# Routing steps of two mixture-of-experts layers inside the stages ahead of them

## The chip, the cores and the metric

The kernel runs on one core of a Trainium2 chip. The metric is the device time of one execution in microseconds (us), the median of several runs.

## The reference

The input is 2 x 2048 tokens of 256 float32 values. Four residual layers follow each other, each on the layer-normalised rows: an attention with 16 heads, a feed-forward, a memory-routed gated linear attention, and the same feed-forward again:

```python
x = x + attn_a(layernorm(x))
x = x + ffn(layernorm(x))
x = x + attn_b(layernorm(x))
x = x + ffn(layernorm(x))
```

The feed-forward is a mixture of 16 experts of inner width 128, two per token, and one shared expert:

```python
shared = silu(x @ ws_gate) * (x @ ws_up) @ ws_down
scores = sigmoid(x @ gate_w.T)
topk_w, topk_idx = top_k(scores, 2)
topk_w = topk_w / (topk_w.sum(-1, keepdims=True) + 1e-20) * 2.5
out = shared + sum over the two of topk_w * expert[topk_idx](x)
```

The last part of attn_b, which the output stage computes, is for each token a sum of two memories' results and the shared one, divided by its root mean square over each head's 64 values, times silu of a gate (x @ w_g), times w_o.

## The kernel before

The tokens are 32 tiles of 128 rows; four tiles (512 tokens) are a step, so a pass over all tokens has 8 steps. The program is a row of stages, one function each, in which every engine has an in-order program of its own; semaphores order them, and all engines meet between two stages. Four stages matter here.

**Merge** (phase_merge, L990) ends attn_a. It works in 16 half-steps of two tiles: PE makes the linear part's outputs, transposes and projects, DVE adds the residual, POOL multiplies the states. Beside it, four steps of rows are already normalised for the feed-forward (DVE L1096 ff., POOL, ACT).

**The feed-forward** (phase_moe, L1181) runs twice: the first time its names begin with m1_ or m_ and four steps (K) come normalised, the second time one (K = 1). Its front goes through the 8 steps. For each, PE transposes the rows (L1584), makes the 16 logits of each row (L1594) and the gate/up product of the shared expert (L1604); ACT copies the transposed rows (L1390), normalises the rows of a later step (L1374), takes silu (L1382) and an exponential (L1396), with a table load ahead of each of the two; DVE picks the two best experts (L1456 to L1487); PE counts the rows ahead in each expert (the ranks, L1615 to L1619); DVE makes the slots (L1490 to L1499); POOL then scatters the rows into the experts' regions in DRAM (L1358). For each token tile and choice there is one indirect store, eight a step, and a step's first waits until all earlier ones have landed:

```python
if n:
    pool.wait_ge(sent, n * G * TOPK * 16)
for t in range(n * G, (n + 1) * G):
    for j in range(TOPK):
        pool.indirect_dma_start(out=xs, ...)
```

When all steps are counted, DVE makes the tables of tiles (L1507 to L1535). Sixteen stores of blank rows fill each region's end, eight issued by SP (L1281) and eight by ACT (L1405), where they stand behind the last silu. Then SP loads the experts' tiles (L1292), after waits for the tables, all scatters and all blank stores, and 79 tiles go through the experts (L1667 to L1689).

**The output stage** (phase_final, L2742) ends attn_b in 8 steps and lies right ahead of the second feed-forward. DVE mixes the rows (L2866, tile fn_o), PE makes the gates (L2923), ACT takes silu of 1024 columns (L2824) and 16 squares with sums (L2831), POOL turns the sums into an inverse root (L2803, L2807), DVE multiplies (L2875, L2883), PE transposes (L2933), ACT copies (L2843), PE projects (L2945), DVE adds to the residual (L2892). Each engine's loop over the steps is written out by hand, with silu and squares two steps ahead. When all is done, the rows of step 0 are normalised: sums on DVE (L2907, L2910), the scaling on POOL (L2809 to L2815), ACT (L2849).

The order of the engines' work is what the program says; no planner is in it.

## Time and profile before

| what | value |
|---|---|
| median of 3 runs | 2501.88 us (2498.71 to 2502.81) |
| profiled execution | 2522.7 us |
| its span | 2521.0 us |
| mean granted PE clock | 0.92 |
| busy PE, PEld | 2123.9 us (84%), 1629.8 us (65%) |
| busy DVE, ACT, POOL | 1816.8 us (72%), 1546.2 us (61%), 1521.3 us (60%) |

The merge takes 1080 to 1141 us of the span, the first feed-forward follows; the output stage goes from 2141 to 2226, the second feed-forward's front from there to 2342 and its experts to the end. Busy shares are averages over stages with different limits, so each stage is read by itself. PE is TensorE, PEld its weight loads, DVE VectorE, ACT ScalarE, POOL GpSimd, SP the engine that only issues transfers.

### The profile page before, as it was taken

The page shows a single profiled execution, that of the slowest core. Times are in us where ns is not written, and L with a number is a line of the kernel's source. Part 1 is how long each engine was busy: PE and PEld are TensorE (multiplying, and loading weights), DVE is VectorE, ACT ScalarE, POOL GpSimd, SP SyncE. Part 2 cuts the span into 40 slices and gives each one's busy share as a digit, 9 for nine tenths or more (in the row PEclk, how much of TensorE's full clock was granted, in tenths as well). Part 3 has the DMA queues.
Part 4 walks back from the last instruction along what each step waited for, and adds up shares of the span by engine and source line. Part 5 has one row for each costly group of instructions (what it writes and reads, how often), then busy time and mean ns, then how long its engine had stood idle before and what let it go on. Part 6 is the DMA issues. An engine that isn't in the chain of part 4 may idle for free. (4 is left out here: it accounts for less than half of the span.)

```text
span 2521.0 us, 107266 instructions
## 1 busy us (share of the span) xinstructions
PE 2123.9 (84%) x43952; PEld 1629.8 (65%) x43952; DVE 1816.8 (72%) x4507; ACT 1546.2 (61%) x3824; POOL 1521.3 (60%) x3168
## 2 busy tenths in 40 slices
PE   8789999999999999988499443899999997876893
PEld 5557777777767777765378342677767765654782
DVE  6689999989989998846355552677777775764456
ACT  5578889988888988824233221566766664653330
POOL 3367778877878887885545365454445444356452
PEclk9989999999999999998799655899999998888896
DMA  6911111111121111134466443111111110733456
GB/s 214 281 53 43 47 48 47 43 50 43 46 76 50 43 43 50 24 127 164 114 216 208 165 159 118 31 52 50 54 49 51 43 35 30 250 147 115 143 149 227
DMA packets 188837, 245.65 MB, mean 97 GB/s; under 512 B 41673, under 2 KB 144982, under 8 KB 187457
## 3 DMA queue, kind: packets, MB, share of 16 engines
q1 hardware_dynamic: 161824, 182.08, 24.1%
...
q14 instruction: 132, 1.07, 0.1%
...
## 5 line engine op out<-in xcount | busy, mean ns | idle before, releaser
L672 ACT ACTIVATE at_E<-at_S,at_mn 128x1024 f32<-128x1024 f32 (+7 forms) x704 | 592.1, 847 | 58.9 <-DVE at_mn L741 45.6
L741 DVE TENSOR_REDUCE at_mn<-at_S 128x1 f32<-128x1024 f32 (+3 forms) x448 | 484.5, 1100 | 6.2 <-PE at_S L851 5.8
L892 PE MATMUL at_pcs<-at_E,at_c 128*32 128x256 f32 (+1 forms) x4864 | 410.6, 339 | 2.5 <-issue 2.4
L851 PE MATMUL at_S<-am_sk,am_sq 96*32 96x512 bf16 (+3 forms) x4608 | 375.3, 348 | 9.3 <-ACT at_E L672 2.3
L609 POOL TENSOR_TENSOR at_kvo<-am_kh,am_vh 128x256 f32<-128x256 f32 x512 | 304.8, 629 | 0.1
L892 PEld LDWEIGHTS at_pcs<-at_E,at_c 128*32 128x32 f32 x4864 | 227.1, 109 | 27.1 <-issue 5.4
L1363 POOL DMA_INDIRECT expert_out<-m_ysb,m_dst x158 | 155.4, 984 | 133.7 <-issue 75.2
L594 POOL TENSOR_TENSOR at_half<-at_half 128x128 f32<-128x128 f32 (+4 forms) x640 | 185.5, 290 | 50.1
L662 ACT ACTIVATE at_Tt<-at_S,at_mn 128x192 f32<-128x192 f32 x512 | 174.1, 431 | 59.9 <-DVE at_mn L729 59.8
L851 PEld LDWEIGHTS at_S<-am_sk,am_sq 96*32 96x32 bf16 x4608 | 146.6, 97 | 81.1 <-ACT at_E L672 31.7
L892 PE MATMUL at_pcs<-at_Tt,at_c 128*32 128x128 f32 x1024 | 177.9, 275 | 0.9 <-issue 0.9
L1675 PE MATMUL m_b<-m_wgu,m_xT 128*128 x632 | 167.9, 389 | 1.3 <-issue 0.8
L2612 PEld LDWEIGHTS gl_S<-gl_X,gl_Y 32*64 32x64 f32 x8448 | 110.4, 133 | 82.1 <-issue 62.5
L729 DVE TENSOR_REDUCE at_mn<-at_S 128x4 f32<-128x768 f32 x128 | 121.7, 951 | 51.3 <-PE at_S L834 50.7
L869 PE MATMUL at_M<-am_ident,at_Tt 128*32 128x64 f32 x8192 | 150.9, 221 | 8.5 <-issue 3.2
L2612 PE MATMUL gl_S<-gl_X,gl_Y 32*64 32x32 f32 (+1 forms) x8448 | 130.6, 226 | 31.7 <-ACT gl_A L2336 16.4
L869 PEld LDWEIGHTS at_M<-am_ident,at_Tt 128*32 128x32 f32 x8192 | 134.0, 110 | 33.2 <-issue 26.8
L1416 ACT ACTIVATE m_sg<-m_b 128x128 f32<-128x128 f32 x158 | 43.8, 277 | 170.7 <-issue 109.0
L672 ACT ACTIVATION_READ_ACCUMULATOR at_E<-at_S,at_mn 128x1 f32 x704 | 144.9, 206 | 0.0
L1675 PEld LDWEIGHTS m_b<-m_wgu,m_xT 128*128 128x128 f32 x632 | 120.2, 194 | 23.5 <-issue 6.8
...
L1550 DVE TENSOR_TENSOR m_hd<-m_sg,m_b 128x128 f32<-128x128 f32 x158 | 45.4, 287 | 109.4 <-ACT m_sg L1416 103.4
...
## 6 DMA issues: line engine op xcount, KB each, us to landing
...
rt_yin<-expert_out SPq DMA_DIRECT2D x7, 1024.0 KB, 12.3
...
```

Source lines behind the costliest of these rows:

```text
L594: pool.tensor_tensor(half[:, :, 0:w], half[:, :, 0:w], half[:, :, w:2 * w], ALU.add).then_inc(s_half, 1)
L609: ins = pool.tensor_tensor(kvo[:, t, 0:DH * DH].rearrange("p (d e) -> p d e", d=DH), k3[:, t, :].unsqueeze(2).to_broadcast([P, DH, DH]), v ...
L662: ins = nc.scalar.activation(Tt[:, q, s, :], S[v % NS_B][:, at:at + TW], ACT.Exp, bias=mn[:, q, s, 0:1], scale=-1.0)
L672: ins = nc.scalar.activation(E[:, at:at + w], S[v % NS_B][:, i * CW:i * CW + w], ACT.Exp, bias=mn[:, q, s, 1 + j:2 + j], scale=-1.0, accum ...
L729: nc.vector.tensor_reduce(mn[:, g % NQ, :, 0].rearrange("p (b s) -> p b s", b=2), S[v % NS_B][:, :].rearrange("p (b c) -> p b c", b=2)[:, ...
L741: nc.vector.tensor_reduce(mn[:, q, :, :].rearrange("p s k -> p (s k)")[:, at[0]:at[0] + 1], S[v % NS_B][:, 0:w], AX.X, ALU.min).then_inc(s ...
L851: ins = nc.tensor.matmul(S[v % NS_B][x, at:at + cw], sq[:, u, t * P + x.start:t * P + x.stop], sk[:, u, c0 + c:c0 + c + cw], start=True, s ...
L869: ins = nc.tensor.matmul(M[x, s * P + e * SEG:s * P + (e + 1) * SEG], Tt[:, q, s, e * SEG + x.start:e * SEG + x.stop], ident[:, e * SEG:(e ...
L892: ins = nc.tensor.matmul(pcs[j * R:(j + 1) * R, cols[0]:cols[1]].rearrange("p (b c) -> p b c", c=P), lhsT, rhs, start=(n, j) not in touche ...
L1363: pool.indirect_dma_start(out=yb.rearrange("t (j d) -> (t j) d", j=TOPK), out_offset=bass.IndirectOffsetOnAxis(ap=dst[:, t, :], axis=0), i ...
L1675: ins = nc.tensor.matmul(bank[4 + t % 2][:, 0:2 * MH], xT[:, t % 2, k, :], wgu[:, k, ds(at, D)], start=(k == 0), stop=(k == KC - 1))
L2612: return nc.tensor.matmul(out, Y[r_h, i % 2, l, u * P + keys:u * P + keys + out.shape[0]], queries, start=True, stop=True)
```

## The change

The routing of a step (logits, exponential, pick, ranks, slots, scatter) and its constants move out of phase_moe into a class Routing, which two stages share. Four numbers say how it is split: routed (steps that the earlier stage routes), ahead (steps that it normalises), begun (steps that it scatters), and turns (the order in which the feed-forward goes through the steps for the shared expert and the routings left).

- Merge routes step 0 and normalises four steps as before, each one iteration earlier; it scatters nothing: (1, 4, 0, turns 1 to 7, then 0).
- The output stage routes steps 0 to 4, normalises 0 to 5 and scatters 0 to 3: (5, 6, 4, turns 5, 6, 0, 7, 1, 2, 3, 4). The second feed-forward routes steps 5, 6, 7 and scatters 4 to 7.
- In the output stage each engine's order changes: the gates product and its silu are split in two halves in three buffers of 512 columns, with work on routed rows between them; the stage also loads the routing weights, which phase_moe did.
- In phase_moe the tables (tables(), the same instructions as before) are made right behind step 7's routing.

```diff
...
+class Routing:
...
+        self.routed, self.ahead, self.begun, self.turns = routed, ahead, begun, turns
...
+    def constants(self, pool):
+        pool.iota(self.iota_i[:, :], pattern=[[1, NE]], base=0, channel_multiplier=0).then_inc(self.made, 1)
...
+    def logits(self, pe, n, rows_T, p_l):
+        if n:
+            pe.wait_ge(self.s_ex, n)
+            pe.wait_ge(self.s_chain, (n - 1) * self.CH + 9)
+        for t in range(GT):
+            for k in range(KC):
+                ins = self.nc.tensor.matmul(p_l[:, t * NE:(t + 1) * NE], rows_T[:, k, t * P:(t + 1) * P], self.gw[:, k, :],
+                                            start=(k == 0), stop=(k == KC - 1))
...
+    def exps(self, act, n, p_l):
+        act.wait_ge(self.s_log, n + 1)
+        if n:
+            act.wait_ge(self.s_chain, (n - 1) * self.CH + 1)
+        self.nc.scalar.activation(self.ex[:, :, :], p_l.rearrange("p (g e) -> p g e", g=GT), ACT.Exp, scale=-1.0
+                                  ).then_inc(self.s_ex, 1)
...
+    def pick(self, dve, n):
...
+        dve.wait_ge(self.s_ex, n + 1)
...
+    def scatter(self, pool, n, a, z):
+        if a == 0:
+            pool.wait_ge(self.s_e2, n + 1)
+            pool.wait_ge(self.s_slot, n + 1)
+            if n:
+                pool.wait_ge(self.sent, n * GT * TOPK * 16)
+        for t in range(n * GT + a, n * GT + z):
+            for j in range(TOPK):
+                pool.indirect_dma_start(out=self.xs, out_offset=bass.IndirectOffsetOnAxis(ap=self.slot[:, t, j:j + 1], axis=0),
+                                        in_=self.hx[:, t, :], in_offset=None).then_inc(self.sent, 16)
...
-                if n >= 8 and n % 2 == 0 and (n - 8) // 2 < K:
-                    scale_of((n - 8) // 2)
+                if n == 3:
+                    rt.constants(pool)
+                if n >= 6 and n % 2 == 0 and n // 2 - 3 < rt.ahead:
+                    scale_of(n // 2 - 3)
...
+                if n >= 6 and n % 2 == 0 and n // 2 - 3 < rt.routed:
+                    turned(n // 2 - 3, 1)
+                if n >= 7 and n % 2 and (n - 7) // 2 < rt.routed:
+                    rt.exps(act, (n - 7) // 2, p_l)
+                if n >= 5 and n % 2 and (n - 5) // 2 < rt.ahead:
...
+                    if k < rt.routed:
+                        turned(k, 0)
...
+                if n >= 8 and n % 2 == 0 and (n - 8) // 2 < rt.routed:
+                    rt.place(dve, (n - 8) // 2, p_c)
                 add_rows(n)
-                if n >= 2 and n % 2 == 0 and n // 2 - 1 < K:
+                if n >= 2 and n % 2 == 0 and n // 2 - 1 < rt.ahead:
                     stats_of(n // 2 - 1)
+                if n >= 7 and n % 2 and (n - 7) // 2 < rt.routed:
+                    rt.pick(dve, (n - 7) // 2)
...
+                k = (n - 8) // 2
+                if n >= 8 and n % 2 == 0 and k < rt.routed:
+                    rt.ranks(pe, k, p_c)
                 if n + 1 < NS:
                     turn(n + 1)
+                k = (n - 5) // 2
+                if n >= 5 and n % 2 and k < rt.routed:
+                    turn_rows(k, 0)
                 project(n)
...
+                if n >= 5 and n % 2 and k < rt.routed:
+                    turn_rows(k, 1)
+                k = (n - 6) // 2
+                if n >= 6 and n % 2 == 0 and k < rt.routed:
+                    if k == 0:
+                        pe.wait_ge(rt.gate_in, 16)
+                    pe.wait_ge(s_rT, KC * (k + 1))
+                    rt.logits(pe, k, rT, p_l)
...
-        SETS = ((1, 2), (2, 4), (4, NS)) if K == 1 else ((4, 6), (6, NS))
+        TURNS = rt.turns
+        SETS = ((K, (K + NS) // 2), ((K + NS) // 2, NS))
...
-            for n in range(NS):
-                if n == 1:
+            for n in range(rt.begun, NS):
+                if n == rt.begun + 1:
                     scale_of(LAST)
                 if n >= K:
                     pool.wait_ge(s_hn, (n + 1 - K) * G)
-                pool.wait_ge(s_e2, n + 1)
-                pool.wait_ge(s_slot, n + 1)
-                if n:
-                    pool.wait_ge(sent, n * G * TOPK * 16)
...
+                rt.scatter(pool, n, 0, G)
...
+            for i, n in enumerate(TURNS):
                 for k in range(KC):
-                    act.wait_ge(s_T, n * KC + k + 1)
-                    if k == 0 and n >= 2:
-                        act.wait_ge(s_gu, n - 1)
-                    nc.scalar.copy(hT[:, u, k, :], p_T[k][:, :]).then_inc(s_hT, 1)
-                if n + 1 < NS and n + 1 >= K and n:
-                    front(n + 1)
-                if n:
-                    silu(n - 1)
-                act.wait_ge(s_log, n + 1)
-                nc.scalar.activation(ex[:, :, :], p_l[:, 0:G * NE].rearrange("p (g e) -> p g e", g=G), ACT.Exp,
-                                     scale=-1.0).then_inc(s_ex, 1)
-                if n == 0 and K == 1:
-                    front(1)
+                    act.wait_ge(s_T, i * KC + k + 1)
+                    if k == 0 and i >= 2:
+                        act.wait_ge(s_gu, i - 1)
+                    nc.scalar.copy(hT[:, i % 2, k, :], p_T[k][:, :]).then_inc(s_hT, 1)
+                if i + 1 < NS and TURNS[i + 1] >= K:
+                    front(TURNS[i + 1])
+                if i:
+                    silu(i - 1)
+                if n >= rt.routed:
+                    rt.exps(act, n, p_log)
             silu(NS - 1)
...
+            for i, n in enumerate(TURNS):
+                if i:
+                    hidden(i - 1)
+                if n >= rt.routed:
+                    rt.pick(dve, n)
+                    rt.place(dve, n, p_rank)
+                if i == 0:
                     for later in range(*SETS[LAST]):
                         stats_of(later)
                 else:
-                    add_shared(n - 1)
...
+                    add_shared(i - 1)
+                if n == NS - 1:
+                    tables()
...
+            for i, n in enumerate(TURNS):
+                pe.wait_ge(s_hT, (i + 1) * KC)
+                if n >= rt.routed:
+                    rt.logits(pe, n, hT[:, i % 2, :, :], p_log)
+                if i + 1 < NS:
+                    turn(i + 1)
+                if i:
+                    shared_down(i - 1)
+                if n >= rt.routed:
+                    rt.ranks(pe, n, p_rank)
+                if n == NS - 1:
+                    pe.wait_ge(rt.s_run, NS)
+                    pe.wait_ge(rt.s_ex, NS)
+                    nc.tensor.matmul(p_l[:, 0:NE], rt.ones_h[:, :], rt.run[:, NS % 2, :], start=True, stop=True
+                                     ).then_inc(s_n, 1)
+                if i == 0:
                     pe.wait_ge(shared_in, 32)
-                if n + 1 < NS:
-                    shared_gu(n)
-            pe.wait_ge(s_run, NS)
-            pe.wait_ge(s_ex, NS)
-            nc.tensor.matmul(p_l[:, 0:NE], ones_h[:, :], run[:, NS % 2, :], start=True, stop=True).then_inc(s_n, 1)
-            shared_gu(NS - 1)
+                shared_gu(i)
...
+            inverse(0)
+            inverse(1)
+            rt.constants(pool)
+            for n in range(1, NS):
+                if n + 1 < NS:
+                    inverse(n + 1)
+                if n - 1 < rt.ahead:
+                    scale_of(n - 1)
+                if 0 <= n - 3 < rt.begun:
+                    rt.scatter(pool, n - 3, 0, G)
...
             for n in range(NS):
                 for k in range(KC):
                     act.wait_ge(s_T, n * KC + k + 1)
                     if k == 0 and n:
                         act.wait_ge(s_zmm, 2 * n)
                     nc.scalar.copy(yT[:, k, :], p_T[:, k, :]).then_inc(s_yT, 1)
+                if 0 <= n - 2 < rt.routed:
+                    rt.exps(act, n - 2, p_l)
                 if n + 2 < NS:
-                    gates(n + 2)
+                    gates(n + 2, 0)
+                if 0 <= n - 1 < rt.ahead:
+                    front(n - 1)
+                if 0 <= n - 1 < rt.routed:
+                    turned(n - 1, 0)
+                    turned(n - 1, 1)
+                if n + 2 < NS:
+                    gates(n + 2, 1)
                     squares(n + 2)
-            act.wait_ge(s_rstd, 4)
-            for a in range(G):
...
             mix(1)
             for n in range(NS):
+                norm(n)
+                if 0 <= n - 3 < rt.routed:
+                    rt.place(dve, n - 3, p_c)
+                if n:
+                    residual(n - 1)
+                    if n - 1 < rt.ahead:
+                        stats_of(n - 1)
                 if n + 1 < NS:
                     gate_rows(n + 1)
-                norm(n)
+                if 0 <= n - 2 < rt.routed:
+                    rt.pick(dve, n - 2)
                 if n + 2 < NS:
                     mix(n + 2)
-                if n:
-                    residual(n - 1)
...
+            for n in range(2):
+                gates(n, 0)
+                gates(n, 1)
             for n in range(NS):
                 turn(n)
+                if 0 <= n - 2 < rt.routed:
+                    if n == 2:
+                        pe.wait_ge(rt.gate_in, 16)
+                    rt.logits(pe, n - 2, rT, p_l)
                 if n + 2 < NS:
-                    gates(n + 2)
+                    gates(n + 2, 0)
                 project(n)
+                if 0 <= n - 1 < rt.routed:
+                    turn_rows(n - 1, 0)
+                    turn_rows(n - 1, 1)
+                if n + 2 < NS:
+                    gates(n + 2, 1)
+                if 0 <= n - 2 < rt.routed:
+                    rt.ranks(pe, n - 2, p_c)
...
-        phase_merge(nc, a["x"], q_full, Y, kvc, q0, x0, wc_s, kv_dram, own, state, keep, hx, 4)
-        phase_moe(nc, Y, tw, a["f_gate"], a["f_wgu"], a["f_wd"], xs, yb, gx, None, "m1_", hx, 4)
+        rt = Routing(nc, shared, "r1_", hx, tw, xs, 1, 4, 0, (1, 2, 3, 4, 5, 6, 7, 0))
+        phase_merge(nc, a["x"], q_full, Y, kvc, q0, x0, wc_s, kv_dram, own, state, keep, hx, rt, a["f_gate"])
+        phase_moe(nc, Y, tw, a["f_wgu"], a["f_wd"], xs, yb, gx, None, "m1_", hx, rt)
...
-        phase_final(nc, Y, hT_dram, o_dram, yb, ident, wg, won, tw_b, hT, hx)
-        phase_moe(nc, Y, tw, a["f_gate"], a["f_wgu"], a["f_wd"], xs, yb, None, a["out"], "m2_", hx, 1)
+        rt = Routing(nc, shared, "r2_", hx, tw, xs, 5, 6, 4, (5, 6, 0, 7, 1, 2, 3, 4))
+        phase_final(nc, Y, hT_dram, o_dram, yb, ident, wg, won, tw_b, hT, hx, rt, a["f_gate"])
+        phase_moe(nc, Y, tw, a["f_wgu"], a["f_wd"], xs, yb, None, a["out"], "m2_", hx, rt)
...
```

ACT in the output stage, before: two steps (fn_p_g are the gates, fn_o the mixed rows, fn_p_T the transposed ones).

```order
L2824 ACTIVATE fn_silu<-fn_p_g 128x1024
L2831 ACTIVATE fn_sq,fn_ss<-fn_o 128x64 x16
L2843 COPY fn_yT<-fn_p_T 128x512 x2
L2824 ACTIVATE fn_silu<-fn_p_g 128x1024
L2831 ACTIVATE fn_sq,fn_ss<-fn_o 128x64 x16
L2843 COPY fn_yT<-fn_p_T 128x512 x2
```

And in the changed kernel, one step from the third on (r_ex is the exponential of the routing, ready_rows are the normalised rows, fn_rT their transposed form):

```order
L2966 COPY fn_yT<-fn_p_T 128x512 x2
L1065 ACT_TABLE_LOAD
L1065 ACTIVATE r_ex<-fn_lc 128x64
L2932 ACT_TABLE_LOAD
L2932 ACTIVATE fn_silu<-fn_p_g 128x512
L2952 ACTIVATE ready_rows<-stream,fn_nbias,fn_rstd 128x256 x4
L2959 COPY fn_rT<-fn_p_T 128x512 x2
L2932 ACTIVATE fn_silu<-fn_p_g 128x512
L2940 ACTIVATE fn_sq,fn_ss<-fn_o 128x64 x16
```

The normalising of a finished step's rows and the copies of their transposes now stand between the first half of silu and the second, with the 16 squares behind; a table load precedes the exponential and the silu behind it.

POOL in the output stage, before: its last two inverses and the scaling.

```order
L2803 TENSOR_SCALAR fn_var<-fn_ss 128x16
L2807 TENSOR_TENSOR fn_inv<-fn_var,fn_half 128x16
L2803 TENSOR_SCALAR fn_var<-fn_ss 128x16
L2807 TENSOR_TENSOR fn_inv<-fn_var,fn_half 128x16
L2809 TENSOR_SCALAR fn_varied<-fn_mv 128x4
L2811 TENSOR_TENSOR fn_rstd<-fn_varied,fn_half 128x4
L2813 TENSOR_TENSOR fn_shift<-fn_mv,fn_rstd 128x4
L2815 TENSOR_SCALAR fn_nbias<-fn_shift 128x4
```

And in the changed kernel, one of the middle steps:

```order
L2908 TENSOR_SCALAR fn_var<-fn_ss 128x16
L2912 TENSOR_TENSOR fn_inv<-fn_var,fn_half 128x16
L2897 TENSOR_SCALAR fn_varied<-fn_mv 128x4
L2899 TENSOR_TENSOR fn_rstd<-fn_varied,fn_half 128x4
L2901 TENSOR_TENSOR fn_shift<-fn_mv,fn_rstd 128x4
L2903 TENSOR_SCALAR fn_nbias<-fn_shift 128x4
L1144 DMA expert_rows<-ready_rows,r_slot 67712x258 x8
```

The scaling, which stood once at the end, stands behind each inverse of the first steps, and eight stores of routed rows follow it; the next inverse comes after them.

## Rows read from the trace of the kernel before

**Rows 1.** Windows view, three stretches: start:end, us, busy (and count) of PE, PEld, DVE, ACT, POOL, ...
```profile
1080.00:1141.00 61.00, 56.66 (x458) 45.40 (x450) 29.45 (x66) 17.64 (x33) 44.87 (x50) 0.94 0.39 130
...
2141.00:2226.00 85.00, 68.77 (x320) 57.81 (x320) 57.01 (x104) 50.12 (x285) 28.60 (x21) 0.91 0.56 186
...
2226.00:2342.00 116.00, 77.82 (x365) 52.21 (x365) 62.78 (x316) 49.50 (x77) 72.24 (x94) 0.82 0.44 153
```

**Rows 2.** Timeline of POOL, second feed-forward: store 1, store 17, store 57, store 64 (start, us)
```profile
2238.61 1.11 POOL L1358 DMA_INDIRECT expert_rows<-ready_rows,m_slot  x1 [4.25 <-DVE m_slot L1499]
...
2265.40 0.96 POOL L1358 DMA_INDIRECT expert_rows<-ready_rows,m_slot  x1 [2.30 <-DMA expert_rows<-ready_rows,m_slot]
...
2326.71 0.96 POOL L1358 DMA_INDIRECT expert_rows<-ready_rows,m_slot  x1 [3.03 <-DMA expert_rows<-ready_rows,m_slot]
...
2335.56 0.96 POOL L1358 DMA_INDIRECT expert_rows<-ready_rows,m_slot  x1 [0.30 <-issue]
```

**Rows 3.** Timeline of SP's and ACT's queues: stage start, ACT's blank stores, first expert load
```profile
2226.39 0.35 SPq L1270 DMA_DIRECT2D m_gw<-in_f_gate  x1
...
2321.65 9.87 ACTq L1405 DMA_DIRECT2D expert_rows<-m_empty  x8
...
2338.79 19.97 SPq L1292 DMA_DIRECT2D m_xg<-expert_rows  x15
```

**Rows 4.** Timeline of PE, second feed-forward: first product, a settled step, the last
```profile
2238.26 5.07 PE L1604 MATMUL m_b<-m_hT,m_wgu 128*128 128x512 f32 x8
...
2259.57 3.68 PE L1604 MATMUL m_b<-m_hT,m_wgu 128*128 128x512 f32 x8
2263.09 1.85 PE L1594 MATMUL m_b<-m_gw,m_hT 128*128 128x16 f32 x16
2264.79 1.07 PE L1584 MATMUL m_b<-m_ident,ready_rows 128*128 128x128 f32 x8
2265.70 1.89 PE L1631 MATMUL m_b<-m_wd,m_hid 128*128 128x256 f32 x8
...
2314.79 0.20 PE L1615 MATMUL m_b<-m_sel,m_tri_h 128*128 128x64 bf16 x1 [3.12 <-DVE m_sel L1479]
...
2315.33 5.38 PE L1604 MATMUL m_b<-m_hT,m_wgu 128*128 128x512 f32 x8
```

**Rows 5.** Timeline of POOL, output stage: inverses of steps 6 and 7, the scaling
```profile
2205.73 0.20 POOL L2803 TENSOR_SCALAR fn_var<-fn_ss 128x16 f32<-128x16 f32 x1 [4.70 <-ACT fn_sq L2831]
2206.01 3.12 POOL L2807 TENSOR_TENSOR fn_inv<-fn_var,fn_half 128x16 f32<-128x16 f32 x1
...
2213.84 0.20 POOL L2803 TENSOR_SCALAR fn_var<-fn_ss 128x16 f32<-128x16 f32 x1 [4.71 <-ACT fn_sq L2831]
...
2221.30 0.25 POOL L2809 TENSOR_SCALAR fn_varied<-fn_mv 128x4 f32<-128x4 f32 x1 [4.27 <-DVE fn_mv L2910]
...
2223.03 0.23 POOL L2815 TENSOR_SCALAR fn_nbias<-fn_shift 128x4 f32<-128x4 f32 x1
```

**Rows 6.** Timeline of ACT, second feed-forward: normalising, silu, table load, exponential
```profile
2250.89 2.08 ACT L1374 ACTIVATE ready_rows<-stream,m_nbias,m_rstd 128x256 f32<-128x256 f32 x4
...
2254.28 0.60 ACT L1382 ACTIVATE m_act_g<-m_b 128x512 f32<-128x512 f32 x1
2254.89 1.28 ACT L1396 ACT_TABLE_LOAD   x1
2256.19 0.22 ACT L1396 ACTIVATE m_ex<-m_b 128x64 f32<-128x64 f32 x1
```

**Rows 7.** Timeline of PE, output stage: gates product and projection
```profile
2172.80 3.62 PE L2923 MATMUL fn_p_g<-ready_wg,ready_hT 128*128 128x256 f32 x16
2176.26 3.62 PE L2945 MATMUL fn_p_z<-ready_won,fn_yT 128*128 128x256 f32 x16
```

**Rows 8.** Tile fn_o: duration ns min/median/max of ACT's squares
```profile
L2831 ACT ACTIVATE fn_sq<-fn_o x128: 238/243/257, 2152.6 to 2213.4; 128x64 f32<-128x64 f32 x128
```

**Rows 9.** Timeline of POOL, first feed-forward: its first scatter
```profile
1154.90 1.22 POOL L1358 DMA_INDIRECT expert_rows<-m_rows,m_slot  x1 [5.57 <-DVE m_slot L1499]
```

476 lines of the change are left out of this document (251 added, 225 removed).

## The prediction

> **What bounds the kernel now.** I read the windows view first, then POOL's timeline in the second feed-forward, then the timelines of its neighbours. The windows [rows 1] are to show where an engine fills its stretch: PE works 56.66 of the merge's 61 us and 68.77 of the output stage's 85, so these two are PE's or nearly so; in the second feed-forward's front nobody fills the time, POOL is busy 72.24 of 116 us and PE 77.82. There an order of waits sets the end.
>
> In the front that order is POOL's [rows 2]. It scatters the rows of one step after the other, eight sets of eight indirect stores. The first store starts at 2238.61, the last at 2335.56; between sets it waits 2.30 us for the earlier ones to land, and from 2265.40 to 2326.71 five sets take 12.26 us each. The expert loads follow at 2338.79, 112.4 us after the stage's start at 2226.39 [rows 3]. They also wait for 16 stores of blank rows; ACT issues half of them, in 9.87 us, and only behind its last silu. They end at 2331.5, under the scatters.
>
> PE works in the same stretch [rows 4]: the first shared gate/up product starts at 2238.26, the last at 2315.33, so a step takes 11.0 us. A settled step is shorter: 3.52 us for the product (2259.57 to 2263.09), 1.70 logits (to 2264.79), 0.91 transposes (to 2265.70), 1.73 down, some 0.8 waiting for the pick (both estimates, from 1.89 less an overlap, and from the step's rest), 0.15 ranks: 8.8. The other 2.2 us a step are waits and a slower clock: after 3.12 us idle the product takes 5.38 us instead of 3.68. The granted clock of the front is 0.82, of the output stage 0.91 [rows 1], so PE spends part of both at the lower level, 1.2 GHz.
>
> In the output stage one step takes 8.11 us (2205.73 to 2213.84) [rows 5]. POOL is idle 4.7 us of it, waiting for ACT's squares; what fills it is PE, with a gates product of 3.46 and a projection of 3.62 [rows 7] and 0.91 for transposes.
>
> **The change, part by part.** First the second feed-forward's front. Four sets leave it, and of the routings three remain (steps 5, 6, 7). POOL needs 4 x 12.26 = 49 us, starting about 4.5 us in, so it ends at 54 and binds nothing. PE takes its place. I leave the first product where it is, 11.9 us in. The seven intervals to the last product: two with routing at 8.8, five without at 3.52 + 0.91 + 1.73 + 0.55 waiting for the hidden rows (an estimate) = 6.7, together 51.1. Of the excess of 2.2 us a step (15.4) I take half, 7.7, because five of seven steps lose the wait for the pick, in which PE cooled. Bounds: none and all of it. Then 3.5 for the product and 0.6 for silu, and now ACT's eight blank stores lie bare: 9.9, and 2.3 to land. First expert load at 11.9 + 51.1 + 7.7 + 16.3 = 87.0 instead of 112.4: **25.4 us gained**, bounds 17.7 and 33.1. So of the 49 us taken off POOL some half comes through; the next lateness is PE's steps and ACT's stores.
>
> Second, the output stage. What matters is not that POOL and ACT have room but the loop that the new order closes. ACT normalises step n-1 (front) ahead of the second half of silu and of the squares of step n+2; POOL takes the inverse of n+2 from those squares, and the scaling, on which the next front waits, stands behind that inverse. One turn of the loop is:
> - inverse 3.40 (2205.73 to 2206.01 + 3.12) and scaling 1.96 (2221.30 to 2223.03 + 0.23) on POOL [rows 5];
> - four normalisations, 2.08 on ACT [rows 6];
> - eight transposes, 0.91 [rows 4], then the second half of the gates product, 3.46 / 2 = 1.73, on PE [rows 7]: in PE's order it stands behind those transposes;
> - silu of 512 columns 0.60 [rows 6], and 16 squares of 0.243 = 3.9 on ACT [rows 8].
>
> That is 14.6, and 14.9 with some seven handovers of 0.05 us. Before, the loop held only squares, inverse, product and transposes, and its step was 8.11. The two copies of 512 columns (0.60 each, as the silu of that width), two table loads, exponential and first silu half (1.2 + 2.56 + 0.22 + 0.60 = 4.6) fit under the inverse and scaling (5.36) and cost nothing; without that cover they would cost 4.6 us a step. POOL's scatter takes 9.81 (2326.71 to 2335.56 + 0.96); it lies beside front to squares (9.3 plus handovers), so it adds little: POOL's own turn is 3.40 + 1.96 + 9.81 = 15.2. Ahead of the routed transposes PE waits for the front some 3 us, by my layout of the step, the length after which it was slow [rows 4]. Then 2.64 us of the loop take up to twice as long. I take 14.9 for the first turn and 16.6 for four; bounds 14.9 and 17.5 for all five. From the inverse of step 2 to that of step 7 are five turns: 81.3 instead of 5 x 8.11 = 40.6, **40.7 us lost**. At the end the last inverse, scaling and scatter take 15.2 and 1.8 to the next stage, 17.0 instead of 12.55 (2213.84 to 2226.39) [rows 3]: 4.4 lost. At the start the constants and the stats of step 0 delay the inverse of step 2 by some 2.2 (bounds 1 and 3). Output stage: **47.3 us lost**, bounds 40 and 55.
>
> The scatter stores share the DMA with the stage's loads, and the mean 0.56 busy share of the stage [rows 1] leaves room; I cost them at nothing. The loads' cover is the longer step itself.
>
> A table load costs 1.28 here, and the next activation starts 0.02 us after it (2254.89 + 1.28, 2256.19) [rows 6]: no wait of its own behind it. The Trainium skill, page "ScalarE: Activation LUTs", section "What ACT_TABLE_LOAD costs", counts a drain of about the load's own length as well, 2.66 us a switch. By the row the two loads cost nothing; by that rule they would overrun their cover, which speaks against the change, and it is a rival below.
>
> Third, merge and first feed-forward. Merge is PE's: 1.70 + 0.91 + 0.15 and 0.7 for waits, 3.5 lost; the constants on POOL lie in the slack between two states (bounds 2.5 and 7). In the feed-forward POOL's first scatter no longer waits 5.57 us for the pick [rows 9]; all eight sets stay, and POOL stays the bound: 5.6 gained (bounds 3 and 10, as ACT's stores now meet other sets). Net **2.1 gained**.
>
> Sum: 47.3 - 25.4 - 2.1 = **+19.8 us**. The profiled execution took 2522.7 us, 0.8% above the median of 2501.88, so it would come to 2542.5; on the median it is 2521.7, and I forecast 2522.
>
> **The rivals.**
> *It comes out even.* The clock stays high in the output stage (14.9 x 5 = 74.5, 33.9 lost, and 4.4 and 1.0 at the ends: 39.3), the front's stalls vanish with the scatters (33.1 gained), and the first half gains 5. Then 39.3 - 33.1 - 5 = +1: 2503. For it: PE would have only short waits outside the one for the front. Against it: that wait is about as long as the one that slowed PE here.
>
> *Faster.* The loop doesn't bind, because squares get ahead by more than a step, and the added work lies beside the old. Then a turn is the busiest engine's: PE 68.77 / 8 + 2.8 + the part at low clock, ACT 50.12 / 8 + 2.08 + 2.56 + 0.22 + 1.2 = 12.3, and POOL 15.2 where it scatters. Two turns of 12.3 and three of 15.2 are 70.2, 29.6 lost, 34.0 with the end; with 33.1 and 7 gained elsewhere: 2496. It decides where the mean turn is below about 14.2 us. Against it: every link waits in an in-order queue.
>
> *Tables.* A switch costs ACT twice what a load shows, 2.56 us instead of 1.28, because the engine empties around it. Then ACT's work under POOL's 5.36 us is 4.6 + 2.56 = 7.2, so 1.8 too long, five times: 9 us more, 2531. Against it: between the end of the normalising (2250.89 + 2.08 = 2252.97) and the silu (2254.28) lie 1.31 us, one load and no more [rows 6]. The page of the Trainium skill named above states such a drain.
>
> *A stall more.* If PE's unexplained 2.2 us a step come with the scatters, four steps of the output stage have them too: 9 more, 2531. This lies in the range.
>
> **How the numbers follow.** Forecast with its own bounds 0.74, tables 0.03, even 0.12, faster 0.11. About 5 us (0.2%) is what a measurement of this kernel can tell from none. The lower end takes the output stage's lower bound with the front's upper and the first half at its best (10 - 2.5 = 7.5 gained): 40 - 33.1 - 7.5 = -0.6, 2501, which takes in the even case. The upper end leaves the first half as forecast: 55 - 17.7 - 2.1 = 35, 2537. What it leaves out is the faster case and a few in 100 of the others. Slower: 0.74 + 0.03 and 0.01 of the even case, 0.78; the same 0.11; faster 0.11.
>
> **What would show it.** In the changed profile: the inverse (fn_inv) of steps 3 to 7 every 15 to 17 us, each waiting for fn_sq; the output stage 130 us long, ending with eight scatters; PE idle about 3 us ahead of the transposes of routed rows; the first expert load of the second feed-forward some 87 us after its start, with ACT's blank stores just ahead of it and POOL long idle; the first feed-forward's first scatter some 6 us in. I am wrong if fn_inv comes every 12 us or less, or if the expert loads start before 75 us.

## The result and the profile after

The changed kernel takes 2523.72 us (median of 4 runs, 2519.0 to 2525.07), the kernel before 2500.88 beside it: 1.0088 times as long, 95% interval 1.0071 to 1.0106, or 22.8 us slower. The forecast was 2522.

The two profiled executions differ by 1 us alone (spans 2521.0 and 2522.0), since the one before was a long one. A second profile of the kernel before (b0, below) has a span of 2499.8 and shows where: 15 us of it lie between the first feed-forward's expert loads and the output stage, which the change does not touch, and 5 in the last experts. All differences below are against this second profile. The stages are cut at rows of the timelines: a feed-forward begins where POOL clears its identity (m_ident) and its front ends with the first expert load, the output stage begins with the first load of fn_o (for merge, that of mg_qT).

| us | merge | first front | between | output stage | second front | last experts |
|---|---|---|---|---|---|---|
| before, first profile | 57.3 | 118.8 | 880.0 | 84.6 | 112.4 | 182.2 |
| before, second profile | 57.6 | 116.5 | 864.8 | 84.8 | 114.9 | 177.2 |
| changed | 67.2 | 110.9 | 862.8 | 138.8 | 80.6 | 175.9 |
| changed less second | +9.6 | -5.6 | -2.0 | +54.0 | -34.3 | -1.3 |

With 1.8 us ahead of merge this is the 22.2 us between the spans. The spread of one stage from profile to profile is of the order of 2.5 us: the output stage, which x2 and m1 below leave as it is, takes 136.2 and 138.3 us there instead of 138.8. The bounds of the last two stages, from SP's timeline of the changed kernel and then of the kernel before (start, duration, engine; the next stage before began at 2207.7):

```profile
2126.74 0.33 SPq L2870 DMA_DIRECT2D fn_o<-o_shared  x1
...
2265.50 0.56 SPq L1448 DMA_DIRECT2D m_wgu<-in_f_wgu  x1
...
2346.12 52.90 SPq L1469 DMA_DIRECT2D m_xg<-expert_rows  x36
```

```profile
2122.90 0.33 SPq L2779 DMA_DIRECT2D fn_o<-o_shared  x1
...
2322.62 6.46 SPq L1292 DMA_DIRECT2D m_xg<-expert_rows  x6
```

POOL's timeline in the output stage of the changed kernel answers to [rows 5]. Each fn_var row is the start of a step's inverse, from step 2 to step 7:

```profile
2161.04 0.32 POOL L2908 TENSOR_SCALAR fn_var<-fn_ss 128x16 f32<-128x16 f32 x1 [8.42 <-ACT fn_sq L2940]
...
2176.76 0.20 POOL L2908 TENSOR_SCALAR fn_var<-fn_ss 128x16 f32<-128x16 f32 x1 [9.52 <-ACT fn_sq L2940]
...
2192.94 1.00 POOL L2908 TENSOR_SCALAR fn_var<-fn_ss 128x16 f32<-128x16 f32 x1 [11.01 <-ACT fn_sq L2940]
2194.02 2.93 POOL L2912 TENSOR_TENSOR fn_inv<-fn_var,fn_half 128x16 f32<-128x16 f32 x1
2196.93 0.24 POOL L2897 TENSOR_SCALAR fn_varied<-fn_mv 128x4 f32<-128x4 f32 x1
...
2199.39 1.11 POOL L1144 DMA_INDIRECT expert_rows<-ready_rows,r_slot  x1 [0.23 <-issue]
...
2202.32 1.62 POOL L1144 DMA_INDIRECT expert_rows<-ready_rows,r_slot  x1 [0.30 <-issue]
...
2210.36 0.93 POOL L2908 TENSOR_SCALAR fn_var<-fn_ss 128x16 f32<-128x16 f32 x1
...
2227.77 0.91 POOL L2908 TENSOR_SCALAR fn_var<-fn_ss 128x16 f32<-128x16 f32 x1
...
2245.18 0.58 POOL L2908 TENSOR_SCALAR fn_var<-fn_ss 128x16 f32<-128x16 f32 x1
```

The five turns take 15.7, 16.2, 17.4, 17.4 and 17.4 us. In the second profile of before the same six lie between these two rows, 8.1 apart:

```profile
2154.60 0.20 POOL L2803 TENSOR_SCALAR fn_var<-fn_ss 128x16 f32<-128x16 f32 x1 [7.55 <-ACT fn_sq L2831]
...
2195.18 0.20 POOL L2803 TENSOR_SCALAR fn_var<-fn_ss 128x16 f32<-128x16 f32 x1 [4.70 <-ACT fn_sq L2831]
```

Two things are to be seen. In the first two turns POOL waits 9.5 and 11.0 us for ACT's squares: it is not the bound there. In the last three no idle time stands behind fn_var: POOL comes from its last store straight to the next inverse, so it is the bound itself. The row at 2192.94 opens such a turn: inverse 3.99 (to 2196.93), scaling 2.46 (to 2199.39), eight stores 10.97 (to 2210.36). Beside two of its long rows DVE runs a product over 1024 columns:

```profile
2192.68 1.20 DVE L3003 TENSOR_TENSOR fn_gated<-fn_o,fn_silu 128x1024 f32<-128x1024 f32 x1
...
2201.88 1.22 DVE L3011 TENSOR_TENSOR fn_y<-fn_gated,fn_inv 128x1024 f32<-128x1024 f32 x1
```

ACT's timeline in the same turn, and PE's in two others, show the other chain:

```profile
2193.82 1.28 ACT L1065 ACT_TABLE_LOAD   x1
2195.12 0.22 ACT L1065 ACTIVATE r_ex<-fn_lc 128x64 f32<-128x64 f32 x1
2195.36 1.28 ACT L2932 ACT_TABLE_LOAD   x1
2196.66 0.60 ACT L2932 ACTIVATE fn_silu<-fn_p_g 128x512 f32<-128x512 f32 x1
2199.20 2.08 ACT L2952 ACTIVATE ready_rows<-stream,fn_nbias,fn_rstd 128x256 f32<-128x256 f32 x4 [1.95 <-POOL fn_nbias L2903]
...
2205.86 0.60 ACT L2932 ACTIVATE fn_silu<-fn_p_g 128x512 f32<-128x512 f32 x1 [2.76 <-PE fn_p_g L3059]
```

```profile
2184.09 1.09 PE L3091 MATMUL fn_p_T<-ready_ident,ready_rows 128*128 128x128 f32 x8 [2.69 <-ACT ready_rows L2952]
2185.03 3.39 PE L3059 MATMUL fn_p_g<-ready_wg,ready_hT 128*128 128x256 f32 x8
...
2218.73 1.38 PE L3091 MATMUL fn_p_T<-ready_ident,ready_rows 128*128 128x128 f32 x8 [3.75 <-ACT ready_rows L2952]
2219.91 3.32 PE L3059 MATMUL fn_p_g<-ready_wg,ready_hT 128*128 128x256 f32 x8
```

ACT waits 1.95 us for the scaling, normalises, and later waits 2.76 us for the second half of the gates product. PE waits 2.69 and 3.75 us for the normalised rows, long after its projection, and then needs 3.4 and 3.3 us for that half, which takes 1.89 at the high clock (2192.41 in x3 below). The granted clock of the stage is 0.86 (0.91 before, [rows 1]), by the windows view:

```profile
2127.00:2265.00 138.00, 93.81 (x465) 78.12 (x463) 86.19 (x279) 79.12 (x337) 76.64 (x81) 0.86 0.44 146
```

In the second front, from PE, ACT's queue and POOL (they answer to [rows 4], [rows 3] and [rows 2]):

```profile
2275.94 6.10 PE L1707 MATMUL m_b<-m_hT,m_wgu 128*128 128x512 f32 x8
...
2324.59 3.60 PE L1707 MATMUL m_b<-m_hT,m_wgu 128*128 128x512 f32 x8
...
2331.45 3.60 PE L1707 MATMUL m_b<-m_hT,m_wgu 128*128 128x512 f32 x8
```

```profile
2335.76 8.05 ACTq L1559 DMA_DIRECT2D expert_rows<-m_empty  x8
```

```profile
2326.11 0.96 POOL L1144 DMA_INDIRECT expert_rows<-ready_rows,r_slot  x1 [0.30 <-issue]
```

PE's last product starts 65.9 us in, a step without routing takes 6.86 us, and POOL is done 19 us ahead of the first load. ACT's blank stores stand last, at 2335.76 to 2343.81.

Merge was the surprise. PE's timeline there:

```profile
1125.64 0.21 PE L1076 MATMUL mg_lc<-r_sel,r_tri_h 128*128 128x64 bf16 x1 [4.20 <-DVE r_sel L1114]
...
1126.72 3.62 PE L1338 MATMUL mg_z<-am_wc,mg_yT 128*128 128x256 f32 x8
...
1131.90 1.89 PE L1338 MATMUL mg_z<-am_wc,mg_yT 128*128 128x256 f32 x8
```

The ranks of step 0 wait 4.20 us for DVE's pick, at the head of PE's queue, with merge's own products behind them, and the projection after it takes 3.62 us instead of 1.89: from 1125.6 to 1130.3 the granted clock is 0.50, the lower of the two levels. The logits, transposes and ranks (2.8 us by my forecast), this wait and the 1.7 us of the slower projection make 8.7. In the first feed-forward POOL's first store comes 7.0 us after the start (forecast 6), but the second set then waits 5.02 us for the first to land:

```profile
1153.02 0.20 POOL L72 MEMSET m_ident<- 128x128 f32 x1 [10.77 <-POOLq L56]
...
1160.02 1.24 POOL L1144 DMA_INDIRECT expert_rows<-m_rows,r_slot  x1 [0.64 <-issue]
...
1177.85 1.09 POOL L1144 DMA_INDIRECT expert_rows<-m_rows,r_slot  x1 [5.02 <-DMA expert_rows<-m_rows,r_slot]
```

### The profile page after: what moved, and what is told of

Read it like the earlier page. It is cut to its first block and busy times, and to the rows that moved or that the text cites. A ratio compares the mean times of both kernels' runs of the same rounds, so it can differ in the third digit from the quotient of the medians.

```text
span 2522.0 us, 107445 instructions
## 1 busy us (share of the span) xinstructions
PE 2123.7 (84%) x44000; PEld 1639.4 (65%) x44000; DVE 1820.3 (72%) x4507; ACT 1550.2 (61%) x3840; POOL 1533.7 (61%) x3184
## 5 line engine op out<-in xcount | busy, mean ns | idle before, releaser
L662 ACT ACTIVATE at_Tt<-at_S,at_mn 128x192 f32<-128x192 f32 x512 | 174.1, 431 | 59.4 <-DVE at_mn L729 59.3
L892 PE MATMUL at_pcs<-at_Tt,at_c 128*32 128x128 f32 x1024 | 177.2, 274 | 0.2
L2698 PEld LDWEIGHTS gl_S<-gl_X,gl_Y 32*64 32x64 f32 x8448 | 108.2, 133 | 67.2 <-issue 46.5
L2698 PE MATMUL gl_S<-gl_X,gl_Y 32*64 32x32 f32 (+1 forms) x8448 | 125.9, 226 | 20.5 <-ACT gl_A L2422 17.1
L827 PE MATMUL at_S<-am_mask,am_identb 128*32 128x384 bf16 x1024 | 101.5, 332 | 26.1 <-PEq L56 16.3
```

The lines of the kernel that those rows point to most:

```text
L662: ins = nc.scalar.activation(Tt[:, q, s, :], S[v % NS_B][:, at:at + TW], ACT.Exp, bias=mn[:, q, s, 0:1], scale=-1.0)
L892: ins = nc.tensor.matmul(pcs[j * R:(j + 1) * R, cols[0]:cols[1]].rearrange("p (b c) -> p b c", c=P), lhsT, rhs, start=(n, j) not in touche ...
L2698: return nc.tensor.matmul(out, Y[r_h, i % 2, l, u * P + keys:u * P + keys + out.shape[0]], queries, start=True, stop=True)
```

## The experiments

Ratios are to runs of the kernel before on the same chip; the changed kernel's is 1.0088. Turns are the distances of the inverses of steps 2 to 7.

### Where the first profile's time was (b0)

> The kernel before, unchanged, for a second profile, since its first profiled execution took 2522.7 us against a median of 2500.9. If the 20 us lie in a stage that the change does not touch, this execution takes about 2501 us and the output stage still lasts 84 to 86 us from its first load to the next stage, the second feed-forward's front 112 us to its first expert load. If they lie in the stages of the change, the one or the other is shorter by up to 20 us, and the gain of the front that I read would be too large.

It took 2501.46 us. The output stage and the second front are 84.8 and 114.9 us, against 84.6 and 112.4. So the first case holds for the output stage; the front was expected at 112 and is 2.5 us longer, so the stages of the change can be compared in either profile within some 2.5 us.

### No scatter in the output stage (x1)

```diff
-        rt = Routing(nc, shared, "r2_", hx, tw, xs, 5, 6, 4, (5, 6, 0, 7, 1, 2, 3, 4))
+        rt = Routing(nc, shared, "r2_", hx, tw, xs, 5, 6, 0, (5, 6, 0, 7, 1, 2, 3, 4))
```

> The change, but the output stage scatters no set (begun 0), all eight go in the second feed-forward. Theory: two chains of about the same length set a turn of the output stage, ACT's loop over front and squares (15.7 and 16.2 us in the turns without scatter) and POOL with a scatter (17.4). Without scatters all five turns take about 16.1: 80.5 instead of 84.1, and the end is some 4 us shorter; the front of the second feed-forward is bound by POOL's eight sets again, its first expert load comes about 105 us in instead of 80.6. Together about 2540 us. Rival: POOL alone sets the turn; without scatters it falls to 12.3 (ACT's own work), the stage loses 27 us and the time is about 2521.

Ratio 1.0184 (1.0164 to 1.0204). The turns are 15.7, 16.0, 17.0, 15.7 and 16.9, together 81.4; the stage is 130.0, the front 113.5. POOL waits for the squares again in the late turns:

```profile
2208.57 1.00 POOL L2908 TENSOR_SCALAR fn_var<-fn_ss 128x16 f32<-128x16 f32 x1 [10.78 <-ACT fn_sq L2940]
```

The turn that ends here (from 2191.56, 17.0 us) is the forecast's loop, link by link: inverse and scaling to 2197.79, normalising to 2199.91, transposes to 2200.89, half product to 2204.05, silu and squares to 2208.5. So without a single scatter the turns stay where they were, within 3 us of 84.1: ACT's loop is nearly as long as POOL's turn, and the rival (POOL alone sets the turn, 12.3 without scatters) falls. The front was 8 us longer than expected; its second set waited 9.2 us for the first to land, where later ones waited 2.3 to 3.8.

### All blank stores on SP (x2)

```diff
-            for e in range(0, NE, 2):
+            for e in range(NE):
                 at = sp.value_load(pad_at[0:1, e:e + 1], min_val=0, max_val=HOME - P)
...
-            for e in range(1, NE, 2):
-                at = act.value_load(pad_at[0:1, e:e + 1], min_val=0, max_val=HOME - P)
-                act.dma_start(xs[ds(at, P), :], empty[:, :]).then_inc(pad_out[1], 16)
```

> The change, but all 16 stores of blank rows are issued by SP, which stands idle from its own eight to the expert loads, and none by ACT behind its last silu. Theory: in the second feed-forward ACT's eight stores (8.05 us, from 2335.76) are what the first expert load waits for; without them it waits for the tables, about 338.5 us minus the end of PE's last product, and comes 7 to 8 us earlier: 2516 us. The first feed-forward is bound by POOL's scatters and does not move. Rival: the stores of SP and POOL's scatters share the DMA engines, the sets of the scatters land later, and nothing is gained: 2523 us.

Ratio 1.0044 (1.0025 to 1.0063), 2514.45 us. The second front fell from 80.6 to 72.0. The step of the prediction that ACT's stores lie bare there is right, and they cost 8.6 us; the rival (nothing gained) falls.

### The new order without routing (x3, y1)

In x3 the output stage routes nothing:

```diff
-        rt = Routing(nc, shared, "r2_", hx, tw, xs, 5, 6, 4, (5, 6, 0, 7, 1, 2, 3, 4))
+        rt = Routing(nc, shared, "r2_", hx, tw, xs, 0, 1, 0, (0, 1, 2, 3, 4, 5, 6, 7))
```

> The change in the first half of the program alone: the output stage routes no step and scatters none, it normalises step 0 only, and the second feed-forward goes through its steps in their own order; the output stage keeps its new order of work and its halved gates. Theory: merge is 10.2 us longer and the first feed-forward's front 8.2 shorter, 2 us lost together; the output stage falls back to within 3 us of 84.6 and the second front to 112: 2503 to 2506 us. Rival: the new order itself costs time in the output stage, without any routing in it (silu in halves, the norm ahead of the gated rows): 10 us or more, 2513 us.

Ratio 1.0121 (1.0102 to 1.0141). The theory fell: the stage takes 106.3 us, 21.5 more than before, with turns of 12.7, 12.5, 12.6, 10.9 and 10.9, though it routes and scatters nothing and normalises one step. PE and ACT in one turn of x3:

```profile
2187.17 5.41 PE L3083 MATMUL fn_p_z<-ready_won,fn_yT 128*128 128x256 f32 x16 [2.84 <-ACT fn_yT L2966]
2192.41 1.89 PE L3059 MATMUL fn_p_g<-ready_wg,ready_hT 128*128 128x256 f32 x8
```

```profile
2194.34 0.60 ACT L2932 ACTIVATE fn_silu<-fn_p_g 128x512 f32<-128x512 f32 x1 [6.73 <-PE fn_p_g L3059]
```

The projection waits for ACT's copies, which stand behind the squares; the second half of the gates product stands behind the projection (2192.41); silu waits for it (6.73 us idle), and the next squares stand behind silu. That is a loop of its own: copies, projection 3.5 (5.2 at the low clock), half product, silu, squares. y1 takes one link out of x3:

```diff
                 if n + 2 < NS:
                     gates(n + 2, 0)
+                    gates(n + 2, 1)
                 project(n)
...
-                if n + 2 < NS:
-                    gates(n + 2, 1)
```

> As the kernel x3_stage_routes_none (the output stage routes nothing and took 106.3 us instead of 84.8), but on PE both halves of the gates product stand ahead of the projection, as the whole product did before. Theory: in x3 a turn is 10.9 us with PE at the high clock and 12.6 at the low one because the second half stands behind the projection, which waits for ACT's copies, which stand behind the squares: copies 0.6, projection 3.5, half product 1.7, silu 0.6, squares 3.9, handovers. With the product ahead, a turn falls to 8.1 to 8.5, the stage to 86 to 90 us, and the time from 2532.7 to 2513 to 2517. Rival: the halved silu and DVE's new order (the norm ahead of the gated rows) are what costs; the stage stays above 100 us and the time above 2525.

Ratio 1.0045 (1.0027 to 1.0062): the stage is 84.2 us, the turns add up to 41.8. So the loop through the projection is shown, and it accounts for the whole 21.5 us of x3. What is left of 1.0045 lies in merge (66.4) and in the second front, which is 121.6 where it was 114.9: its first store comes 17.7 us in instead of 11.8. The later steps are normalised there in two groups instead of three (SETS in the diff); whether that is the reason was not tried.

### Opening the loop, badly (y2, y3, y4)

In y2 PE's halves are as in y1, ACT normalises ahead of the exponential and takes both silu halves ahead of the copies of the routed transposes, and on POOL the scaling stands ahead of the inverse:

```diff
             for n in range(1, NS):
-                if n + 1 < NS:
-                    inverse(n + 1)
                 if n - 1 < rt.ahead:
                     scale_of(n - 1)
+                if n + 1 < NS:
+                    inverse(n + 1)
```

> The change with its loop opened: PE makes both gates halves ahead of the projection, ACT normalises right behind the copies (ahead of the exponential and silu) and POOL's scaling stands ahead of the inverse, so that neither front nor squares waits for the inverse of the same turn. Four sets are scattered as before. Theory of two chains: the first two turns fall from 15.7 and 16.2 to about 12.5, ACT's own work, the three with scatters stay at POOL's 17.4: 7 us gained, 2517. Rival (ACT's loop sets all turns): all five fall to 12.5 and the time is 2503.

y3 adds a division of three sets over the turns:

```diff
+                head = {3: (0, 3), 4: (1, 2), 5: (2, 1)}
+                tail = {4: (0, 3), 5: (1, 2), 6: (2, 1)}
+                if n in tail:
+                    rt.scatter(pool, tail[n][0], tail[n][1], G)
...
+                if n in head:
+                    rt.scatter(pool, head[n][0], 0, head[n][1])
```

> As y2_loop_open, but the output stage scatters only three sets, three token tiles (six stores) in each of four turns instead of four. Theory of two chains: POOL's turn is 3.4 + 2.0 + 6 x 1.27 = 13.0 and ACT's 12.1, so a turn takes 13 to 13.5, five of them 66 instead of 84; the end is 5 us shorter, since the last scatter no longer outlasts PE; the fifth set in the second feed-forward is hidden there, since POOL ended 20 us ahead of the first expert load: 2523.7 - 18 - 5 = about 2501 us. Rival: the turns stay above 15 because PE at the low clock, or transposes that share a buffer, set them: 2511 or more.

Ratios 1.0095 (1.0075 to 1.0115) and 1.0088 (1.0064 to 1.0112): nothing gained, and both forecasts were misses. Both have turns of 10.7 and then four of exactly 18.4. From POOL, ACT and DVE in one turn of y3:

```profile
2202.32 1.11 POOL L2897 TENSOR_SCALAR fn_varied<-fn_mv 128x4 f32<-128x4 f32 x1 [0.76 <-DVE fn_mv L3032]
```

```profile
2205.19 2.07 ACT L2956 ACTIVATE ready_rows<-stream,fn_nbias,fn_rstd 128x256 f32<-128x256 f32 x4 [3.22 <-POOL fn_nbias L2903]
...
2208.58 0.23 ACT L1065 ACTIVATE r_ex<-fn_lc 128x64 f32<-128x64 f32 x1
```

```profile
2212.05 3.38 DVE L2998 SCALAR_TENSOR_TENSOR fn_o<-fn_yin,ready_tw_b,fn_o 128x256 f32<-128x256 f32 x8
2215.35 1.22 DVE L3015 TENSOR_TENSOR fn_y<-fn_gated,fn_inv 128x1024 f32<-128x1024 f32 x1
...
2217.46 1.28 DVE L3024 TENSOR_TENSOR stream<-fn_p_z,stream 128x512 f32<-128x512 f32 x2
```

```profile
2220.69 1.11 POOL L2897 TENSOR_SCALAR fn_varied<-fn_mv 128x4 f32<-128x4 f32 x1 [0.76 <-DVE fn_mv L3032]
```

The scaling is released by DVE's stats (fn_mv), the normalising by the scaling, the exponential stands behind it, DVE's pick waits for the exponential, the mix (2212.05) stands behind the pick, then come norm, slots, residual (2217.46) and the next stats. From one scaling to the next (2202.32 to 2220.69) the links follow each other without a gap: 2.9 us scaling, 2.1 normalising, 1.6 table load and exponential, 3.2 pick, 3.3 mix, 2.1 norm and slots, 3.2 residual and stats. One loop was opened and another closed, 18.4 us long, whatever POOL scatters: in both runs the first of the four long turns, between the inverses of steps 3 and 4, holds no store at all. My division was a miss too: between two inverses of the other three there still lay eight stores. That this loop sets the turns is read from the rows; no run takes one link out of it alone. y4 is y3 with x2's blank stores and no routing in merge:

> As y3_open_three_spread, with all 16 blank stores on SP (worth 9.3 us alone) and no routing in merge. Theory: the blank stores give 5 us here, less than 9.3, since POOL's five sets end about 76 us in; merge becomes 9 us shorter and the first feed-forward's front 5.5 us longer, 3.5 gained: about 2492 us, faster than both kernels. Rival: POOL's longer row of sets takes the whole gain of the blank stores, and the constants alone are what made merge longer: 2501 us.

Ratio 1.0047 (1.0034 to 1.0061), 2510.01 us where I had forecast 2492. The output stage is the same (138.4), the second front 75.0, merge and first front together 171.8 instead of 178.3 in y3.

### Orders written for what each engine waits for (z1, z2, z3)

ACT's loop in z1 (PE makes projection, ranks, both gates halves and then the routed transposes; DVE the residual and stats ahead of the slots and the mix ahead of the pick):

```diff
                     nc.scalar.copy(yT[:, k, :], p_T[:, k, :]).then_inc(s_yT, 1)
                 if 0 <= n - 2 < rt.routed:
                     rt.exps(act, n - 2, p_l)
                 if n + 2 < NS:
-                    gates(n + 2, 0)
+                    squares(n + 2)
                 if 0 <= n - 1 < rt.ahead:
                     front(n - 1)
+                if n + 2 < NS:
+                    gates(n + 2, 0)
                 if 0 <= n - 1 < rt.routed:
                     turned(n - 1, 0)
                     turned(n - 1, 1)
                 if n + 2 < NS:
                     gates(n + 2, 1)
-                    squares(n + 2)
```

> The change with the same five, six and four steps, but the output stage's orders written anew: ACT does copies, exponential, squares of n+2, normalising, first silu half, copies of the routed transposes, second half; PE the projection ahead of both gates halves, the routed transposes last; DVE the mix ahead of the pick. So the squares wait for the mixed rows alone, and no chain leads from the inverse over normalising, transposes and gates back to them. Theory (order, not amount, costs the stage): the turns before the first scatter are 6 to 11 us, the three with a scatter are POOL's own 3.4 + 2.0 + 10.9 = 16.3, the stage lasts 116 us instead of 138.8 and the time is 1.0088 - 0.0092 = 0.9996 of before. Rival (amount costs it: ACT's and POOL's added work): turns without scatter stay above 13, the stage above 130, the ratio above 1.005.

Ratio 1.0028 (1.0013 to 1.0042). The stage takes 123.6 us, the same routed, normalised and scattered steps as in the changed kernel, 15.2 less. The turns without a scatter fell from 15.7 and 16.2 to 11.3 and 11.2; those with one are 17.1, 18.9 and 17.5. This order, which changes three engines' programs at once, gives back 15.2 of the 54 us; which of its moves counts was not taken apart. Of the 38.8 us left, 29.1 lie in the three turns with a scatter, 7.6 at the stage's end and 6.4 in the two turns without; the start is 4.3 shorter. In the first of the scatter turns POOL has waited 5.63 us for the squares, and comes to the next inverse straight from its stores:

```profile
2172.66 0.73 POOL L2908 TENSOR_SCALAR fn_var<-fn_ss 128x16 f32<-128x16 f32 x1 [5.63 <-ACT fn_sq L2940]
...
2189.79 0.20 POOL L2908 TENSOR_SCALAR fn_var<-fn_ss 128x16 f32<-128x16 f32 x1
```

So most of the rest goes with POOL's stores. The result lies between the theory (116 us, 0.9996) and the rival (over 130 us and 1.005), and neither holds: I had priced the three scatter turns at 16.3 each, 4.6 us too little.

z2 and z3 do less in the output stage, with merge's routing undone and the blank stores on SP. ACT's order is z1's, but both make gates products ahead of the projection on PE (in z1 they stand behind it). They differ from each other in two places of the output stage's orders: z3's PE makes both gates halves ahead of the ranks (z2's has the ranks between them), and its DVE multiplies the gated rows ahead of the residual. And they differ in the line of numbers, z2's and then z3's:

```diff
+        rt = Routing(nc, shared, "r2_", hx, tw, xs, 2, 3, 2, (2, 3, 4, 5, 6, 0, 7, 1))
...
+        rt = Routing(nc, shared, "r2_", hx, tw, xs, 4, 4, 3, (0, 4, 5, 6, 7, 1, 2, 3))
```

> Orders as in z1_squares_first (on DVE the slots first, on POOL the scatter ahead of the scaling), but the output stage routes and scatters two steps and normalises three, all blank stores are SP's, merge routes nothing. Theory: output stage 95 us (84.8 before), since only two of POOL's turns hold a scatter; second front 87 us (114.9 before), six sets of POOL's; merge and first front 2 us shorter together: 17 to 20 us faster than before, 0.993. Rival: what POOL doesn't scatter in the output stage it scatters in the front at the same price, and the front's start is longer with six steps to normalise: no gain, 1.000.

> As z2_two_steps, but the output stage routes and normalises four steps and scatters three. Theory: output stage 107 us, second front 75: 182 together against 199.7 before, and 2 from the first half: 0.992. It differs from z2 by one more set in the output stage (12 us there, 12 saved in the front), so the two should stand within 2 us; where they differ by more, the loop of the order counts after all.

z2: 0.9968 (0.9956 to 0.9981), output stage 97.9, second front 95.6. z3: 0.9927 (0.9905 to 0.9948), 2479.69 us, output stage 108.0, second front 76.0. z3 is faster than both kernels, and the forecast of 0.992 holds. z2's 0.993 was a miss.

In z3 the two stages add up to 184.0 us, against 199.7 before and 219.4 in the changed kernel. It changes amount, orders, merge and blank stores at once, and their shares were not taken apart. Its first expert load comes 12.15 us after the start of POOL's last set, the length of a set with its landing:

```profile
2289.30 0.96 POOL L1144 DMA_INDIRECT expert_rows<-ready_rows,r_slot  x1 [3.41 <-DMA expert_rows<-ready_rows,r_slot]
```

```profile
2301.45 123.06 SPq L1468 DMA_DIRECT2D m_xg<-expert_rows  x79
```

z2's front is 8.6 us longer than I expected. From POOL and SP:

```profile
2304.23 0.96 POOL L1144 DMA_INDIRECT expert_rows<-ready_rows,r_slot  x1 [0.30 <-issue]
```

```profile
2290.61 18.49 SPq L1458 DMA_DIRECT2D expert_rows<-m_empty  x16
2311.63 5.89 SPq L1468 DMA_DIRECT2D m_xg<-expert_rows  x6
```

Its first store comes 15.3 us into the front (2231.32), and the last of its six sets ends at 2305.19. With some 2.3 us to land, an estimate from the waits between sets, the first load could not come before 2307.5, 91.5 us in. SP can store the blank rows only when step 7 is counted, which z2 does second to last; they take 18.49 us, end at 2309.10, and the load comes at 2311.63. So some 4 of the 8.6 us lie with the blank stores and the rest with POOL's sets.

The two kernels were to stand within 2 us, and z3 is 10 us faster. Its output stage is 10.1 us longer and its front 19.6 shorter: the first store comes 8.4 us earlier (6.9 us in instead of 15.3), from the first set's start to the last's it takes 7.1 less, with one set fewer, and 4.1 less lie behind the last set's start. That is read from the rows; since the output stage's orders differ as well, no run separates these causes.

### Merge alone (m1)

```diff
-        rt = Routing(nc, shared, "r1_", hx, tw, xs, 1, 4, 0, (1, 2, 3, 4, 5, 6, 7, 0))
+        rt = Routing(nc, shared, "r1_", hx, tw, xs, 0, 4, 0, (0, 1, 2, 3, 4, 5, 6, 7))
```

> The change with one part undone: merge routes no step (the first feed-forward routes all eight, steps in their own order); merge still normalises four steps early and makes the constants. Theory: merge's routing is what made the stage 9.7 us longer (PE stood 4.2 us before the ranks, waiting for DVE's pick, with its own states' work queued behind, and the projection after it ran at half clock): merge falls from 67.2 to about 58.5, the first feed-forward's front rises from 110.9 by 1.5 to 5.6: 3 to 7 us gained, ratio 1.006 to 1.0075. Rival (my forecast's sizes: 3.5 in merge against 5.6 in the front): the time rises by 2 us, 1.0095.

Ratio 1.0083 (1.0068 to 1.0099), not to be told from 1.0088. Merge fell from 67.2 to 58.4, the first front rose from 110.9 to 119.0. So one routed step costs merge 8.8 us and gives the front 8.1: nothing is gained or lost. Both sizes were larger than my forecast's 3.5 and 5.6, and neither theory's total was right. With no routing in merge, merge and first front still take 177.4 us together against 174.1 (second profile) and 176.1 (first) before; what the change leaves there besides (constants and normalising earlier) was not tried by itself.

## Why the prediction came out right

| term | forecast | measured |
|---|---|---|
| five turns, against 40.6 | 81.3 | 84.1 |
| start of the output stage | +2.2 | +2.6 |
| its end | +4.4 | +7.8 |
| output stage | +47.3 | +54.0 |
| second front | -25.4 | -34.3 |
| merge | +3.5 | +9.6 |
| first front | -5.6 | -5.6 |
| sum | +19.8 | +22.8 (medians) |

The stages' differences do not add up to the last row: they come from two profiles, it from the medians.

**The loop of the output stage** is there, with nearly the forecast length: in x1, where no scatter lies in it, a turn is 15.7 to 17.0, within the stated 14.9 to 17.5. I had PE slow in four turns of five. In x1 the half product takes 3.16 us in the turn of 17.0 (granted clock 0.90) and 1.89 in the turn of 15.7 (1.00), so a turn at the high clock is 0.8 us longer than the 14.9 I gave it. But "so it adds little", of the scatter, was too weak, and the sign "each waiting for fn_sq" held only in the two turns without one. In the three with one POOL itself is the bound, 1.1 us above x1's mean of 16.3: I had 15.2 for its own work and it needs 17.4, because its stores take 10.97 instead of 9.81, the inverse with its fn_var 3.99 instead of 3.40 and the scaling 2.46 instead of 1.96. That term was mis-sized by 2.2 us in three turns, and the last set at the stage's end likewise (20.3 us from the last inverse, forecast 17.0).

**What I missed there** is that the new order costs 21.5 us even with nothing added (x3), by a second loop through the projection. I wrote that before, product and transposes were in the loop; that the second half of the product had moved behind the projection I did not follow. It did not show in the total, because the loop over the normalising is longer and covers it: in the changed kernel the half product waits for the routed transposes, and PE stands 3.75 us ahead of those with its projection done (2218.73). That is read from the rows; y1's edit was not tried on the changed kernel.

**The rival "faster"** put the turns at 12.3 by ACT's work. z1 shows that it was no wrong idea for the turns without a scatter: with orders in which the squares do not wait for silu they are 11.2 and 11.3. With a scatter they are 17.1 to 18.9, where the rival had 15.2, so z1 is not faster than before. **Tables**: the two loads take 1.28 us each, and the activations follow 0.02 us later (2195.12, 2196.66); no further wait. The Trainium skill, page "ScalarE: Activation LUTs", section "What ACT_TABLE_LOAD costs", counts a drain as well; these rows do not show one. **Even** had 14.9 a turn and 5 gained in the first half: its front came true (34.3 gained), the other two did not. **A stall more** put 9 us into the output stage; 6.7 are there, but in POOL's turns and at the end.

**The second front** was right in its mechanism (PE's steps 6.86 against 6.7 forecast, then ACT's stores, POOL long done) and mis-sized in three small terms: the first product came 10.4 us in, not 11.9; the seven intervals took 55.5 and not 58.8, with a granted clock of 1.00 from 2290 to 2335; and 14.7 instead of 16.3 lay behind the last product. Against the first profile the gain is 31.8, inside my bounds; against the second 34.3, just outside, as its baseline is 2.5 us longer.

**Merge** is the step that failed: "0.7 for waits". The ranks stood 4.20 us at the head of PE's queue, and the projection behind them ran at the lower clock. By m1 the routed step costs merge 8.8 us and not 3.5, and gives the front 8.1 and not 5.6, so it loses 0.7 where I had 2.1 gained. The net of the first half against the second profile is a loss of 4.0; the other 3.3 us are not the routing's, and between the two profiles of before alone this sum differs by 2.0.

So the total is within 3 us partly because errors cancel: 6.7 too little in the output stage and 6.1 in merge, 8.9 too little gain in the second front.
